# The first feed-forward's first layer moved into the last attention batch of a two-layer gated cross-attention kernel

## The chip, the cores and the metric

The kernel runs on one core of one Trainium2 chip. The time is the device time of the whole launch, in microseconds, as the median of several runs. Profiled executions give a trace of every instruction of the engines: TensorE (PE, its weight loads PEld), VectorE (DVE), ScalarE (ACT), GpSimd (POOL) and the DMA queues.

## The reference, cut to what matters

Four residual blocks run one after the other on x (8 batches of 100 tokens, 256 wide). Only the first block is touched here:

```
xn  = layernorm(x)
q   = xn @ Wq + bq                       # 16 heads of 16
k,v = ctx @ Wk + bk, ctx @ Wv + bv       # ctx: 8 x 361 x 192
out = softmax(q k^T / 4) v               # 8 x 100 x 256
h   = relu(out @ W1 + b1)                # 256 -> 512
x   = x + tanh(g) * (h @ W2 + b2)        # 512 -> 256
```

After it come a mixture of 8 experts with top-1 routing, a cross-attention with ternary weights and int8-rounded activations on the same context, and a mixture of 16 attention projections. The context projections of the third block don't depend on x. Two of their layers are woven into the attention rounds of the first block as "chain units".

## The kernel before, in words

Every engine's stream is written out by hand, in one order, with semaphores between the engines. All matrices named here are fp32.

The attention of the first block runs in ten rounds, n = 0 to 9 (`for n in range(B + 2)`, once in the ACT block and once in the PE block). Round n works on batch n: `turn_maxima(n)` turns the row maxima, and then twelve steps u take one group of four heads and a third of the context each. At even u the PE runs `score_pair(n, u)` (four fp32 products at L1761 and two bf16 ones at L1767) for steps u and u + 1, and where `EXTRA[n]` has one a `chain_unit` (L1704 in round 7). ACT turns each step's scores into probabilities with an exponential (L1414). Scores, chain units and the turned maxima share three banks, so the PE may only be three results ahead of ACT. At u = 6 and 10 the PE computes `values(n - 1, ..)` of the batch before (L1779) into bank 7. ACT copies that bank at its own u = 10 (`zo`, L1409), the PE turns it (`turn_values(n - 1)`, L1791), DVE divides by the sums (`normalise`, L750 and L751), the PE turns the result back in the next round at u = 2 (`turn_heads(n - 2)`, L1798), and ACT adds the bias and stores it in `qT` (`heads_out`, L1380). `values(b)` waits for `heads_out(b - 1)`.

Rounds 8 and 9 have no scores of their own. Only values and turns of the last batches are left in them.

The feed-forward follows. `first_product(half, m)` is the first layer for four batches (half 0: batches 0 to 3) and a quarter m of the 512 hidden columns: two k-steps of 128x400 in fp32, four instructions in the trace (L1608, weights from `w_1`, seen as `region` and `w_a`). `hidden_out(n)` is ACT's relu of it into `h0T` (L1390). `second_layer(b)` is the second layer for one batch: four k-steps of 100x256, eight instructions (L1608, `stage<-stage`, seen as `bank<-stage`), into bank b % 4. From b = 4 on it waits for `x1_done` b - 3, which is DVE's residual of batch b - 4.

In the kernel before, the four `first_product(0, m)` and their `hidden_out` stand in rounds 8 and 9 between the turns. `second_layer(0)` stands behind round 9. Then the PE waits for the last `heads_out`, runs `first_product(1, 0..3)` and then `second_layer(1)` to `second_layer(7)`, with `turn_tokens_half(2, 0)` (L1602) after `second_layer(6)`.

On DVE, the order after round 8's `normalise(7)` is fixed: the scale of the third block's activations (L723, a reduction over partitions on POOL, L625 to L632), the rounding of the whole context (`quantise(qc, ctx_a, ctx_a, 8)`, L642 and L643 on 128x5776), the bias of the residual (L834), and only then, batch after batch:

```
for b in range(B):
    dve.wait_ge(S["y0_mm"], b + 1)
    dve.scalar_tensor_tensor(x[:, b, :], psum[b % 4]..., x[:, b, :]).then_inc(S["x1_done"], 1)
    dve.wait_ge(S["x1_done"], b + 1)
    ins = token_stats(b)
```

(L838 and L556.) After b = 3 it computes the variance of the first half. ACT normalises those four batches (L1283), the PE turns them, and so on to the router.

`h0T` lies over the part of the stage tile in which the projected values of earlier batches lie. Its first 400 columns touch those of batch 6, whose `values` are run in round 7.

Of the kernel before, what the change touches and what calls it, by code (L numbers as in the profile page):

```python
# [17 lines left out]
B, N, D = 8, 100, 256  # L18
# [119 lines left out]
def flamingo(nc, d):  # L138

    ctx = ExitStack()  # L140
    with ctx:
# [3 lines left out]
        def sem(name):  # L145
            return ctx.enter_context(nc.semaphore(name))
# [34 lines left out]
        def raw(name):  # L181
            p, w, _ = TERN[name]
            home = stage if name == "f1" else region
            return home[0:p, RAW[name]:RAW[name] + w]

        def weight(name):
            p, w, at = TERN[name]
            return tern[0:p, at:at + w]
# [67 lines left out]
        def cut_r(n):  # L256
# [62 lines left out]
        S = {n: sem(n) for n in (  # L319
            "small_in", "x_in", "raw_in", "ctx_in0", "ctx_in1", "ctx_in2", "ctx_in3", "ctx_in4", "consts_in", "w_q_in", "ffn_in", "w_abs", "tern_ready",  # L320
            "ln_var", "ln_std", "ln_out", "ln_turned", "xT_ready",
            "max_part", "max_all", "quantised", "kv_mm", "kv_out", "xn_stored", "placed", "inverse_mm", "inverse_done", 
            "q_mm", "q_out", 
            "pv_mm", "o_out",
            "h0_mm", "h0_out", "y0_mm", "x1_done",
            "logit_mm", "logit_a", "logit_e", "onehot_done", "rank_mm", "te_done", "zeroed",
            "w1_in0", "w1_in1", "w2_in0", "w2_in1", "xs_in0", "xs_in1", "xs_turned", "xs_out",
# [932 lines left out]
        def _(act):  # L1260
# [82 lines left out]
            def f1_magnitude(part):  # L1343

                at_p = slice(1024 * part, 1024 * part + 1024)
                if part == 0:
                    act.wait_ge(S["large_in"], 16)
                act.activation(weight("f1")[:, at_p], raw("f1")[:, at_p], ACT.Abs,
                               accum_out=scol[:, 48 + part:49 + part]).then_inc(S["large_abs"], 1)
# [26 lines left out]
            def heads_out(b):  # L1376

                act.wait_ge(S["f_mm"], b + 1)
                for k in range(2):
                    act.activation(qT[:, k, b * N:(b + 1) * N], psum[7][:, k * N:(k + 1) * N], ACT.Identity,  # L1380
                                   bias=cols[:, COLS["bv"] + k:COLS["bv"] + k + 1]).then_inc(S["o_out"], 1)
# [4 lines left out]
            def hidden_out(n):  # L1386

                half, m = n // 4, n % 4
                act.wait_ge(S["h0_mm"], n + 1)
                act.activation(h0T[:, m, half * HT:(half + 1) * HT], psum[n][:, 0:HT], ACT.Relu,  # L1390
                               bias=cols[:, 4 + m:5 + m]).then_inc(S["h0_out"], 1)

            for n in range(B + 2):
                if n < B:
                    act.wait_ge(S["y_mm_a"], FIRST[n] + 1)
                    act.copy(nmT[n % 2], psum[4 + FIRST[n] % 3][:, 0:200].bitcast(BF16)).then_inc(S["y_out_a"], 1)
                if n == B:
                    hidden_out(0)
                if n == B + 1:
                    hidden_out(2)  # L1400
                    hidden_out(3)
                for u in range(12):
                    if u == 2 and n >= 2:
                        heads_out(n - 2)
                    if u == 4 and n == B:
                        hidden_out(1)
                    if u == 10 and 1 <= n <= B:
                        act.wait_ge(S["pv_mm"], n)
                        act.copy(zo, psum[7][:, 0:4 * N]).then_inc(S["zo_out"], 1)  # L1409
                    if n < B:  # L1410
                        c, g = u // 4, u % 4
                        rows_c, y = CH[c][1], UNIT[n, u]
                        act.wait_ge(S["y_mm_a"], y + 1)
                        act.activation(probsT[n % 2][0:rows_c, c, g].rearrange("p j n -> p (j n)"),  # L1414
                                       psum[4 + y % 3][0:rows_c, 0:4 * N], ACT.Exp).then_inc(S["y_out_a"], 1)
                        if u % 2 == 1 and u // 2 < len(EXTRA[n]):
                            chain_out(*EXTRA[n][u // 2])
                        if (n, u) in TOTAL:
                            total_out(n, u)
                        if n == 3 and u % 3 == 2:  # L1420
                            f1_magnitude(u // 3)

            for n in range(4, 8):
                hidden_out(n)
# [148 lines left out]
        def _(pe):  # L1573
# [32 lines left out]
            def layer(bank, w, src, halves, kk, start=True, stop=True):  # L1606
                for k in range(kk):
                    ins = pe.matmul(bank, w(k), src(k), start=start and k == 0, stop=stop and k == kk - 1)  # L1608
                return ins
# [114 lines left out]
            def score_wave(b, w):  # L1724

                t, par = w // 2, w % 2
                if w == 0:
                    pe.wait_ge(S["qm_done"], b + 1)
                for i in range(4):
                    if (b, w, i) == (0, 1, 2):  # L1730
                        pe.wait_ge(S["sum_read"], 1)
                    if 4 * b + w > 0 and i % 2 == 0:
                        pe.wait_ge(S["x_max"], 2 * (4 * b + w - 1) + i // 2 + 1)
                    at_i = slice(32 * i, 32 * i + 32)
                    ins = pe.matmul(psum[i + (4 if b == 0 else 0)][0:N, 0:M], qm[b % 3][at_i, t, 2 * (i % 2) + par, :], kT[at_i, t, b, :],  # L1735
                                    start=True, stop=True)
                    if i % 2 == 1:
                        ins.then_inc(S["x_mm"], 1)
# [78 lines left out]
            def first_product(half, m):  # L1817

                at_h = slice(half * HT, (half + 1) * HT)
                layer(psum[4 * half + m][:, 0:HT], lambda k: w_1[k][:, m * P:(m + 1) * P], lambda k: qT[:, k, at_h], 2, 2)\  # L1820
                    .then_inc(S["h0_mm"], 1)

            def second_layer(b):

                if b >= 4:
                    pe.wait_ge(S["x1_done"], b - 3)
                layer(psum[b % 4][0:N, 0:D], lambda k: h0T[:, k, b * N:(b + 1) * N],
                      lambda k: w_2[:, k, :], 1, 4).then_inc(S["y0_mm"], 1)

            for n in range(B + 2):  # L1830
                if n + 1 < B:
                    score_wave(n + 1, 0)
                if n < B:
                    turn_maxima(n)
                if n == B:
                    pe.wait_ge(S["ffn_in"], 32)
                    pe.wait_ge(S["x_max"], 8 * B)
                    first_product(0, 0)
                if n == B + 1:
                    first_product(0, 3)  # L1840
                for u in range(12):
                    if u == 2 and n >= 2:
                        turn_heads(n - 2)
                    if u == 4 and n + 1 < B:
                        score_wave(n + 1, 1)
                    if u == 4 and n == B:
                        first_product(0, 1)
                    if u in (6, 10) and 1 <= n <= B:
                        values(n - 1, u // 2 - 3)
                        values(n - 1, u // 2 - 2)  # L1850
                    if u in (6, 8) and n + 1 < B:
                        score_wave(n + 1, u // 2 - 1)
                    if n < B and u % 2 == 0:
                        score_pair(n, u)
                        if u // 2 < len(EXTRA[n]):
                            chain_unit(*EXTRA[n][u // 2])
                        if (n, u + 1) in TOTAL:
                            total_unit(n, u + 1)
                if n == B:
                    first_product(0, 2)  # L1860
                if 1 <= n <= B:
                    turn_values(n - 1)
            pe.wait_ge(S["h0_out"], 4)
            pe.wait_ge(S["w1_small_in"], 16)
            second_layer(0)

            pe.wait_ge(S["o_out"], 2 * B)
            for m in range(4):
                first_product(1, m)
            for b in range(1, B):  # L1870
                if b == 4:
                    pe.wait_ge(S["h0_out"], 8)
                second_layer(b)
                if b == 6:
                    turn_tokens_half(2, 0)
# [120 lines left out]
            for n in range(2 * B + 4):  # L1996
                if n < 2 * B:
                    a, b = n // B, n % B
# [24 lines left out]
                if n >= 4:  # L2023
                    g = n - 4
                    a, b = g // B, g % B
# [251 lines left out]
```

## Time and profile before

| | us |
|---|---|
| median of 3 runs | 611.55 (610.88 to 611.57) |
| the profiled execution | 610.34 |
| its span | 608.5 |
| PE busy in the span | 591.6 (97%) |
| DVE busy | 325.9 (54%) |
| ACT busy | 218.4 (36%) |

Times in the profile count from the span's start. Round 7 is at 166.7 to 179.9, rounds 8 and 9 at 179.9 to 189, the rest of the feed-forward up to 209. A timeline row merges neighbouring instructions of one kind. Its start and the start of the next row are exact, while the duration of a PE row includes the drain of its last matmul, so that two rows overlap by some 0.1 to 0.2 us. A busy PE may still stand waiting between two such matmuls.

### The profile page before, as it was taken

The page shows a single profiled execution, that of the slowest core. Times are in us where ns is not written, and L with a number is a line of the kernel's source. Part 1 is how long each engine was busy: PE and PEld are TensorE (multiplying, and loading weights), DVE is VectorE, ACT ScalarE, POOL GpSimd, SP SyncE. Part 2 cuts the span into 40 slices and gives each one's busy share as a digit, 9 for nine tenths or more (in the row PEclk, how much of TensorE's full clock was granted, in tenths as well). Part 3 has the DMA queues.
Part 4 walks back from the last instruction along what each step waited for, and adds up shares of the span by engine and source line. Part 5 has one row for each costly group of instructions (what it writes and reads, how often), then busy time and mean ns, then how long its engine had stood idle before and what let it go on. Part 6 is the DMA issues. An engine that isn't in the chain of part 4 may idle for free.

```text
span 608.5 us, 9623 instructions
## 1 busy us (share of the span) xinstructions
PE 591.6 (97%) x3759; PEld 405.6 (67%) x3759; DVE 325.9 (54%) x787; ACT 218.4 (36%) x511; POOL 75.9 (12%) x75
## 2 busy tenths in 40 slices
PE   9999999999999999999999889999999999999997
PEld 7656344454556777999999558677655555555587
DVE  1996767597876655222222779886362223131454
ACT  3554665756663364121112476662200010001000
POOL 0052201013006203222221000001001000000000
PEclk9999999999999969999999999999999999999999
DMA  8920000102001644999996000601733833220000
GB/s 185 301 107 1 18 1 1 37 2 57 1 1 39 227 169 132 336 345 330 335 341 226 15 2 12 231 2 27 245 101 89 310 104 93 89 78 1 0 28 27
DMA packets 25580, 70.63 MB, mean 116 GB/s; under 512 B 5255, under 2 KB 13031, under 8 KB 21703
## 3 DMA queue, kind: packets, MB, share of 16 engines
q1 hardware_dynamic: 21910, 58.16, 29.3%
q0 software_dynamic: 3632, 11.97, 6.0%
q8 instruction: 25, 0.41, 0.3%
q14 instruction: 13, 0.10, 0.0%
HBM read 64.62 MB, written 5.49 MB: 115 GB/s over the span
## 4 chain that ended last, share of the span: by engine, by line
PE 85%; DVE 6%; ACT 5%; DMA 2%; issue 1%; SPq 1%; POOL 0%; DVEq 0%
PE bank L2112 21%; PE bank L1608 10%; PE bank L1932 8%; PE bank L1945 8%; PE bank L1761 7%; PE bank L2148 7%; PE bank L1735 5%; PE bank L1779 3%; DMA region<-in_ctxT 2%; PE bank L1704 2%; ACT region L1500 2%; PE bank L1767 2%; PE bank L2066 1%; PE bank L1589 1%; DVE nmax L1033 1%
## 5 line engine op out<-in xcount | busy, mean ns | idle before, releaser
L2112 PE MATMUL bank<-region,kvT 128*128 128x400 f32 x384 | 130.4, 500 | 0.0
L2112 PEld LDWEIGHTS bank<-region,kvT 128*128 128x128 f32 x384 | 72.5, 190 | 54.1 <-issue 0.3
L731 DVE TENSOR_REDUCE nmax<-bank 100x2 f32<-100x722 f32 x64 | 55.2, 905 | 24.2 <-PE bank L1735 23.9
L1174 DVE TENSOR_TENSOR region<-xT,stage 128x800 f32<-128x800 f32 x30 | 29.7, 991 | 70.1 <-PE bank L2112 70.0
L1932 PEld LDWEIGHTS bank<-stage,region 128*128 128x128 f32 x448 | 52.1, 192 | 1.4 <-issue 0.8
L1932 PE MATMUL bank<-stage,region 128*128 128x128 f32 x448 | 52.4, 276 | 0.5 <-ACT stage L1435 0.5
L1945 PE MATMUL bank<-region,stage 128*128 128x256 f32 x224 | 50.7, 380 | 0.0
L1945 PEld LDWEIGHTS bank<-region,stage 128*128 128x128 f32 x224 | 41.5, 190 | 5.0
L2148 PE MATMUL bank<-region,kvt 128*128 128x200 f32 (+1 forms) x192 | 44.5, 389 | 0.3 <-DVE region L1200 0.3
L1458 ACT ACTIVATE stage<-bank,stage 128x128 f32<-128x128 f32 x56 | 16.0, 368 | 67.5 <-PE bank L1932 36.5
L2148 PEld LDWEIGHTS bank<-region,kvt 128*128 128x128 f32 x192 | 33.5, 190 | 9.3 <-DVE region L1200 0.6
L1761 PE MATMUL bank<-xT,kvt 64*121 64x400 f32 (+1 forms) x144 | 38.2, 545 | 0.7 <-ACT region L1414 0.4
L947 DVE TENSOR_SCALAR stage<-bank,stage 128x128 f32<-128x128 f32 x56 | 15.8, 345 | 43.1 <-PE bank L1932 43.1
L1200 DVE TENSOR_TENSOR region<-region,stage 128x200 f32<-128x200 f32 (+1 forms) x48 | 20.5, 435 | 31.3 <-PE bank L2148 31.3
L1414 ACT ACTIVATE region<-bank 121x400 f32<-121x400 f32 (+1 forms) x48 | 21.6, 501 | 20.7 <-PE bank L1767 20.7
L1414 ACT ACTIVATE kvT<-bank 121x400 f32<-121x400 f32 (+1 forms) x48 | 21.8, 501 | 18.1 <-PE bank L1767 18.1
L953 DVE TENSOR_TENSOR stage<-bank,stage 128x256 f32<-128x256 f32 x14 | 5.9, 425 | 35.7 <-PE bank L1945 35.7
L1735 PE MATMUL bank<-kvt,xT 32*100 32x361 f32 x192 | 23.6, 502 | 0.7 <-ACT stage L1305 0.5
L1608 PE MATMUL bank<-region,w_a 96*128 96x361 f32 x64 | 21.2, 475 | 1.6 <-DMA region<-in_ctxT 0.9
L1761 PEld LDWEIGHTS bank<-xT,kvt 64*121 64x121 f32 (+1 forms) x144 | 13.4, 178 | 14.0 <-ACT region L1414 3.6
L1536 ACT ACTIVATE region<-bank 128x400 f32<-128x400 f32 x6 | 2.6, 504 | 55.5 <-PE bank L2112 55.5
L1608 PE MATMUL bank<-w_a,region 96*121 96x256 f32 (+1 forms) x96 | 22.1, 381 | 0.0
(352 smaller groups left out, 931.7 us busy)
## 6 DMA issues: line engine op xcount, KB each, us to landing
region<-in_e_w SPq DMA_DIRECT2D x28, 1024.0 KB, 5.8
kvT<-in_p_qkv SPq DMA_DIRECT2D x32, 384.0 KB, 3.1
stage<-w_dram POOLq DMA_DIRECT2D x2, 1600.0 KB, 12.7
stage<-in_t_f SPq DMA_DIRECT2D x1, 2048.0 KB, 15.6
kvt<-in_p_o SPq DMA_DIRECT2D x1, 2048.0 KB, 10.1
stage<-in_e_b SPq DMA_DIRECT2D x14, 128.0 KB, 7.9
region<-in_ctxT SPq DMA_DIRECT2D x3, 541.5 KB, 14.9
stage<-w_dram POOLq DMA_DIRECT2D x1, 1200.0 KB, 8.8
```

What stands on the lines that cost most here:

```text
L731: dve.tensor_reduce(nmax[:, b % 2, at_h:at_h + 9:8], banks[0:N, bank:bank + 2, 0:M], AX.X, ALU.max, negate=True)\
L1174: dve.tensor_tensor(x_w[n % NW], xT[:, :, at_h], w_bc[h][:, None, e, :].to_broadcast([P, 2, HT]), ALU.mult).then_inc(S["xw_done"], 1)
L1200: dve.tensor_tensor(z_w[n % NW][:, at_p], oT[h][:, at_p], w_bc[h][:, e, at_p], ALU.mult)\
L1414: act.activation(probsT[n % 2][0:rows_c, c, g].rearrange("p j n -> p (j n)"), psum[4 + y % 3][0:rows_c, 0:4 * N], ACT.Exp).then_inc(S["y_o ...
L1608: ins = pe.matmul(bank, w(k), src(k), start=start and k == 0, stop=stop and k == kk - 1)
L1735: ins = pe.matmul(psum[i + (4 if b == 0 else 0)][0:N, 0:M], qm[b % 3][at_i, t, 2 * (i % 2) + par, :], kT[at_i, t, b, :], start=True, stop= ...
L1761: pe.matmul(bank[g], kT[at_g, t, b, c0:c0 + rows_c], qm[b % 3][at_g, t].rearrange("p j n -> p (j n)"), start=True, stop=False)
L1779: ins = pe.matmul(psum[7][32 * i:32 * i + VW, w * N:(w + 1) * N], v_b[b][0:rows_c, c, 8 * t + 2 * i + par, :], probsT[b % 2][0:rows_c, c, ...
L1932: ins = pe.matmul(psum[2 * u + m // 4][:, (m % 4) * P:(m % 4 + 1) * P], e_w1[u][:, k, m * P:(m + 1) * P], xsT[u][:, k, :], start=k == 0, s ...
L1945: ins = pe.matmul(psum[4 + u][:, 0:D], hsT[u][:, m, :], e_w2[u][:, m, :], start=m == 0, stop=m == KF - 1)
L2112: ins = pe.matmul(psum[3 * h + j][:, 0:HT], p_w[n % NP][:, k, j * HE:(j + 1) * HE], x_w[n % NW][:, k, :], start=e == 0 and k == 0, stop=e ...
L2148: ins = pe.matmul(psum[LAST_BANK[part] + m][:, at_p], o_all[:, e, m * P:(m + 1) * P], z_w[n % NW][:, at_p], start=e == 0, stop=e == E1 - 1)
```

## The change

The four `first_product(0, m)` move from rounds 8 and 9 into round 7: one after `turn_maxima(7)`, the others at u = 4, 6 and 8 ahead of the step's values and scores. Their `hidden_out` move into ACT's round 7: 1 at u = 6, 2 at u = 8, 0 after the copy of bank 7 at u = 10, and 3 after the last step. In their old places stand `second_layer(0)` to `second_layer(3)`. Behind round 9 the PE runs `first_product(1, 0..3)` and then only `second_layer(4)` to `second_layer(7)`.

```diff
 # ACT
-                if n == B:
-                    hidden_out(0)
-                if n == B + 1:
-                    hidden_out(2)
-                    hidden_out(3)
                 for u in range(12):
                     if u == 2 and n >= 2:
                         heads_out(n - 2)
-                    if u == 4 and n == B:
+                    if u == 6 and n == B - 1:
                         hidden_out(1)
+                    if u == 8 and n == B - 1:
+                        hidden_out(2)
                     if u == 10 and 1 <= n <= B:
                         act.wait_ge(S["pv_mm"], n)
                         act.copy(zo, psum[7][:, 0:4 * N]).then_inc(S["zo_out"], 1)
+                    if u == 10 and n == B - 1:
+                        hidden_out(0)
...
+                if n == B - 1:
+                    hidden_out(3)
 # PE
-                if n == B:
+                if n == B - 1:
                     pe.wait_ge(S["ffn_in"], 32)
                     pe.wait_ge(S["x_max"], 8 * B)
                     first_product(0, 0)
+                if n == B:
+                    pe.wait_ge(S["h0_out"], 4)
+                    pe.wait_ge(S["w1_small_in"], 16)
+                    second_layer(0)
                 if n == B + 1:
-                    first_product(0, 3)
+                    second_layer(3)
                 for u in range(12):
                     if u == 2 and n >= 2:
                         turn_heads(n - 2)
                     if u == 4 and n + 1 < B:
                         score_wave(n + 1, 1)
+                    if u in (4, 6, 8) and n == B - 1:
+                        first_product(0, u // 2 - 1)
                     if u == 4 and n == B:
-                        first_product(0, 1)
+                        second_layer(1)
...
                 if n == B:
-                    first_product(0, 2)
+                    second_layer(2)
                 if 1 <= n <= B:
                     turn_values(n - 1)
-            pe.wait_ge(S["h0_out"], 4)
-            pe.wait_ge(S["w1_small_in"], 16)
-            second_layer(0)
 
             pe.wait_ge(S["o_out"], 2 * B)
             for m in range(4):
                 first_product(1, m)
-            for b in range(1, B):
-                if b == 4:
-                    pe.wait_ge(S["h0_out"], 8)
+            pe.wait_ge(S["h0_out"], 8)
+            for b in range(4, B):
                 second_layer(b)
                 if b == 6:
                     turn_tokens_half(2, 0)
```

## Rows read from the trace of the kernel before

**Rows 1.** The page, part 1: busy us, share of the span, instructions.

```profile
PE 591.6 (97%) x3759; PEld 405.6 (67%) x3759; DVE 325.9 (54%) x787; ACT 218.4 (36%) x511; POOL 75.9 (12%) x75
```

**Rows 2.** The chain that ended last, from round 9 on: start us, us, what.

```profile
188.52 0.60 ACT stage L1390
...
189.17 17.70 PE bank L1608 x72
```

**Rows 3.** Timeline of PE in round 7: start us, us, instructions [idle before].

```profile
167.01 1.23 PE L1761 MATMUL bank<-xT,kvt 64*121 64x400 f32 x3
...
168.67 0.48 PE L1704 MATMUL bank<-stage,tern 128*128 128x361 bf16 x2
...
169.25 1.24 PE L1761 MATMUL bank<-xT,kvt 64*121 64x400 f32 x4
...
170.59 0.48 PE L1704 MATMUL bank<-stage,tern 128*128 128x361 bf16 x2
...
171.09 0.99 PE L1761 MATMUL bank<-xT,kvt 64*121 64x400 f32 x3
...
172.52 0.48 PE L1704 MATMUL bank<-stage,tern 128*128 128x361 bf16 x2
...
174.10 0.94 PE L1761 MATMUL bank<-xT,kvt 64*121 64x400 f32 x4
...
175.13 0.48 PE L1704 MATMUL bank<-stage,tern 128*128 128x361 bf16 x2
...
175.79 0.99 PE L1761 MATMUL bank<-xT,kvt 64*119 64x400 f32 x3 [0.17 <-ACT kvT L1414]
...
177.21 1.25 PE L1779 MATMUL bank<-region,stage 121*17 121x100 f32 x48
...
179.42 0.65 PE L1791 MATMUL bank<-consts,kvT 128*100 128x128 f32 x4
```

**Rows 4.** Timeline of ACT at the end of round 7 and in round 9.

```profile
178.52 0.49 ACT L1409 COPY kvT<-bank 128x400 f32<-128x400 f32 x1 [0.46 <-PE bank L1779]
179.52 0.90 ACT L1414 ACTIVATE kvT<-bank 119x400 f32<-119x400 f32 x2 [0.51 <-PE bank L1767]
...
189.01 0.57 ACT L1380 ACTIVATE xn<-bank,cols 128x100 f32<-128x100 f32 x2
```

**Rows 5.** Timeline of PE in rounds 8 and 9 and behind them.

```profile
179.90 0.84 PE L1608 MATMUL bank<-xn,region 128*128 128x400 f32 x2
...
186.54 0.60 PE L1791 MATMUL bank<-consts,kvT 128*100 128x128 f32 x4
...
190.97 0.84 PE L1608 MATMUL bank<-xn,region 128*128 128x400 f32 x2
...
196.35 10.52 PE L1608 MATMUL bank<-stage 128*100 128x256 f32 x48
```

**Rows 6.** Timeline of DVE, ACT and PE from the rounding of the context on.

```profile
189.82 3.22 DVE L642 TENSOR_SCALAR region<-region,scol 128x5776 f32<-128x5776 f32 x1
...
198.74 0.48 DVE L838 SCALAR_TENSOR_TENSOR x<-bank,tg,x 100x256 f32<-100x256 f32 x1
...
201.73 0.48 DVE L838 SCALAR_TENSOR_TENSOR x<-bank,tg,x 100x256 f32<-100x256 f32 x1 [0.35 <-PE bank L1608]
...
203.97 2.07 ACT L1283 ACTIVATE xn<-x,var,rstd 100x256 f32<-100x256 f32 x4 [0.44 <-DVE var L587]
...
207.40 1.89 PE L1608 MATMUL bank<-stage 128*100 128x256 f32 x8
```

**Rows 7.** Windows: us, busy (x instructions) of PE, PEld, DVE, ACT, POOL, granted PE clock, DMA share, GB/s.

```profile
210.39:213.80 3.41, 1.58 (x11) 0.94 (x10) 1.36 (x7) 2.21 (x6) 0.00 (x0) 1.00 0.84 286
213.80:217.20 3.40, 3.39 (x19) 3.09 (x20) 0.45 (x3) 1.25 (x1) 0.00 (x0) 0.50 0.74 259
217.20:220.60 3.40, 3.40 (x17) 2.63 (x16) 1.84 (x10) 2.15 (x6) 0.00 (x0) 0.50 0.83 303
220.60:224.05 3.45, 3.45 (x15) 2.49 (x14) 3.08 (x21) 2.73 (x6) 0.00 (x0) 0.50 0.25 90
346.90:350.30 3.40, 2.99 (x12) 2.18 (x13) 2.53 (x9) 2.47 (x7) 0.35 (x1) 0.50 0.00 0
```

## The prediction

> **What bounds the kernel now.** I first read the page for the engines' shares: the PE is busy 97% of the span and DVE 54% [rows 1]. So PE work that only changes its place costs what it cost before, unless it lands in a stretch where the PE stands waiting. What matters is where it waits, before and after. Next I read the chain that ended last. From round 9 on it is PE alone except for one ACT relu: 17.70 us of L1608 in one piece, which is seven second layers and four first products [rows 2]. Third, I read the timelines of PE, ACT and DVE around the change, since a busy PE row can hide a wait between two matmuls. There the reader is to see two things. First, in round 7 the PE is held up for short times by ACT, though the page calls it busy. Second, DVE starts its long rounding right behind round 8 and comes to the first residual only at 198.74 [rows 6].
>
> **Two chains start at turn_values(7).** It ends at 187.14 in round 8 (186.54 + 0.60) [rows 5]. One chain is the PE's: first_product(0, 3), turn_heads(7), eight second layers, four first products and one turn of tokens, 22.15 us until second_layer(7) ends at 209.29 (207.40 + 1.89) [rows 6]. The other is DVE's: normalise(7), the scale, 2 x 3.2 us of rounding, the bias, then the residuals of batches 0 to 3, their variance, ACT's normalisation, the turn of tokens and second_layer(7). Before, the PE's chain is the later one, and the DVE's has little slack. The first residual starts 11.60 us behind turn_values(7). The fourth starts at 201.73 after 0.35 us of waiting for the PE, and, counting back the rest of its delay, could have started 0.4 us earlier at the pace of 0.86 us a batch. ACT's four normalisations end at 206.04 (203.97 + 2.07) [rows 6], and would end at 205.6. The turn of tokens needs about 0.45 us behind the last of them, so second_layer(7) could start at 206.1 instead of 207.40. **The slack of DVE's chain is 1.3 us.** Whatever delays turn_values(7) by more than that makes the kernel slower, however much the PE's tail behind it shrinks.
>
> **Part 1, four first products into round 7.** The four of half 1 run back to back from 190.97 to 196.35, so 5.38 us, 1.35 each [rows 5]. What they can fill is the waiting in round 7. A score pair without a wait takes 1.03 us from its first matmul to the next kind (174.10 to 175.13). Pair 0 takes 1.66 (+0.63), pair 2 1.34 (+0.31), pair 4 1.43 (+0.40). Pair 8 starts 0.26 late (0.40 after the chain unit at 175.13 would be 175.53) and takes 1.42, so +0.65 [rows 3]. That is 1.99 us in the round. Three of the four products stand right ahead of pairs 0, 4 and 8 and give ACT the time it lacked there, so I take 1.68 as filled. The 0.31 of pair 2 stays, and first_product(0, 2), ahead of values and pair 6, has no wait to fill. ACT's three relus at u = 6, 8 and 10 cost it 0.5 to 0.6 us each [rows 2]. It has that time, as the PE gives it 1.35 us more at each place. Cost: 5.38 - 1.68 = **+3.70**. Bounds: all 1.99 filled gives +3.4; nothing filled gives +5.4.
>
> **Part 2, second_layer(0) waits for hidden_out(3).** It stands in first_product(0, 0)'s old place, which started at 179.90 right behind turn_values(6) [rows 5]. It needs all four quarters of the hidden layer, and the last relu is queued on ACT behind both last exponentials. ACT copies bank 7 at 178.52 (0.49), then runs the new hidden_out(0) (to 179.50). The exponentials start at 179.52 as before and end at 180.42 [rows 4], and hidden_out(3) ends at 181.02. So the PE, which waited for nothing here, waits from 179.90 to 181.05: **+1.15**. Behind the wait stand turn_heads(6), heads_out(6) and with it values(7). Bounds: 0.9 if ACT's operations run closer, 1.3 if the exponentials come later. The 0.51 us wait of the old second_layer(0) goes away, but it lay behind turn_values(7) and buys nothing on DVE's chain.
>
> **Part 3, second layers for first products in round 8.** Six second layers take 10.52, 1.75 each [rows 5]. Three of them, 0 to 2, stand ahead of turn_values(7) where three first products of 1.35 stood: 3 x 0.40 = **+1.2**. They cover the same hand-overs (normalise(6) to turn_heads(6), the copy of bank 7) with room to spare, so no wait comes or goes.
>
> **Sum at turn_values(7):** 3.70 + 1.15 + 1.2 = 6.05. It ends at 193.2 instead of 187.14.
>
> **Part 4, the tail.** Behind it the PE now has second_layer(3) 1.75, turn_heads(7) 0.17, a wait for heads_out(7) of about 0.6 (its 0.57 [rows 4] no longer lies under second_layer(0)), and four first products 5.38: 7.9 us. Then it waits for h0_out 8 (0.6), and then second_layer(4) waits for x1_done 1, which comes 12.1 us behind turn_values(7) (11.60 + 0.48) [rows 6]. So **the PE stands idle for 4.2 us**, at about 201.1 to 205.3. Before, second_layer(1) to (3) covered this. The end is then DVE's chain: second_layer(7) ends at 209.29 + 6.05 - 1.3 = 214.0, **+4.75 us**. Second layers 4 to 6 run from 205.3 to 210.5, and the turn of tokens isn't ready before 211.7, so they have 1.2 us to spare. Everything behind (router, experts) starts from that end and moves with it. The DMAs of expert weights start from the end of the rounding and from x1_done 8, so they move too, and come no later relative to their users.
>
> **Part 5, the clock.** In the trace the granted clock fell from 1.00 to 0.50 (2.4 to 1.2 GHz) at 213.80, after 3.41 us in which the PE was busy 1.58 us, and stayed there for 10.25 us, of short router products first. After another fall it was back in 3.4 us, at 350.3, under denser work [rows 7]. An idle stretch of 4.2 us is worse than what went ahead of these falls, so I expect a third one, around second_layer(4). Each us at half clock is half a us of PE work. For about 2 us it is lost in the 1.2 us to spare. If it lasts 5.5 us it costs 2.7 - 1.2 = 1.5, and if it lasts as long as the one at 213.80, the rest of the feed-forward doubles: 6.9 + 0.7 us more, less 1.2, so about +6. Weighing these by how dense fp32 second layers are, nearer to the fall at 346.90, I take **+0.5**. (The Trainium skill, TensorE: Matmul & The Clock Gate, in its part on the HAM clock gate, says that the throttled state is the default and that only recent activity releases it. By that rule the fall is certain, and the sum would be 4.75 plus 1 to 2 us. The rows agree on the fall after sparse work. No row has an idle stretch as long.)
>
> **The time.** 610.34 + 4.75 + 0.5 = 615.6 for an execution like the profiled one. The median of the runs lies 1.2 above that one, so 616.8.
>
> **Rivals.**
>
> *A, the same chain, but a long fall of the clock.* The place and the price are those of part 5: +3.5 to +6 above the warm sum, so 619.8 to 622.5. For it: the fall at 213.80 lasted 10.25 us. Against it: those were router products of 8 columns. Chance 0.13.
>
> *B, a smaller loss.* Round 7's fillable waits are larger than I read them, for instance because ACT's delays spread over every pair, and hidden_out(3) is earlier: 3.4 + 0.9 + 1.2 - 1.3 = 4.2 with the counted waits, and with another us filled 3.2, so 614.7, and no fall of the clock. Chance 0.12.
>
> *C, on the other side: the new products cost the PE nothing in round 7.* If ACT and not the PE set the pace of round 7, the four products would slip into its shadow. Then turn_values(7) comes 1.2 later by the second layers alone, which is DVE's slack, the result is 611.5, and without the wait for hidden_out(3) it would be slightly faster. It decides at a delay of turn_values(7) below 1.3 us, for which 5.38 us would have to vanish, against 1.99 us of waits that I can find [rows 3]. If DVE's chain were not the end, the PE would only lose its waits: 2 us filled and 0.5 saved against 1.15, 0.6 and 0.6 new ones, so 611.4. Chance of both together 0.05, split between same and faster.
>
> **How the numbers follow.** The forecast (PE delay of 6.05, DVE's chain as the end, clock fall short) has 0.70 and spans 615.3 to 618.8: 3.9 to 5.9 for the sum by the bounds of parts 1 and 2, and 0 to 1.5 for the clock. With B and half of A the range that holds 8 in 10 is 614.5 to 620.0. About 0.2% (1.2 us) is what a measurement of this kernel can tell from no change. Slower by more has 0.70 + 0.13 + 0.12 = 0.95, within it 0.03, faster 0.02.
>
> **What the profile after would show.** Round 7 from turn_maxima to the end of turn_values(6) is 3.7 us longer, with pairs 0, 4 and 8 at about 1.03. A PE wait of about 1.1 us ahead of second_layer(0) on ACT L1390. L750 of batch 7 at about 193.2. A PE wait of about 4 us ahead of second_layer(4), put down to DVE x L838 (this is the row that tells most). L838 without waits for batches 0 to 3, 0.86 apart. The chain through DVE L642, L643, L834, L838 where PE L1608 stood. A granted clock of 0.5 beginning between 203 and 207. I am wrong if turn_values(7) comes less than 1.3 us later, or if the wait ahead of second_layer(4) is missing. The size is off if the clock stays down longer than some 5 us.

## The result, and the profile after

The changed kernel takes 618.72 us (median of 4 runs, 617.41 to 621.20) against 611.21 us before (4 runs, 609.76 to 611.57). The ratio is 1.0123, with a 95% interval of 1.0097 to 1.0149: 7.5 us slower. The profiled execution took 617.41 us with a span of 615.6 us, 7.1 us longer than before.

The page of the changed kernel, part 1 and the clock row of part 2. The engines' busy time hardly moved (PE 591.6 to 594.2, [rows 1]), so it gives no hint of where 7 us went. The clock row gives one: ahead of the 6 that the row before had too (the fall of 213.80 [rows 7]) there is now a 7, for the slice from 200.1 to 215.5 us. The two 8s further right are the fall that stood at 346.90 before. It lasted 6.83 us here instead of 3.41, and as long in e1 below, which takes the time of the kernel before, so it is not the loss.

```profile
PE 594.2 (97%) x3759; PEld 406.4 (66%) x3759; DVE 325.7 (53%) x787; ACT 218.4 (35%) x511; POOL 76.6 (12%) x75
...
PEclk9999999999999769999999889999999999999999
```

The timeline of PE in the changed kernel (start us, us, instructions, idle before it). Round 7 starts with the turned maxima at 167.09. Every score pair (L1762) now runs without a wait except the one at 170.47.

```profile
167.09 0.34 PE L1749 MATMUL bank<-ident_bf,small 100*128 100x100 bf16 x4
167.27 0.90 PE L1609 MATMUL bank<-xn,region 128*128 128x400 f32 x2
...
168.77 0.94 PE L1762 MATMUL bank<-xT,kvt 64*121 64x400 f32 x4
...
169.81 0.48 PE L1705 MATMUL bank<-stage,tern 128*128 128x361 bf16 x2
...
170.47 0.99 PE L1762 MATMUL bank<-xT,kvt 64*121 64x400 f32 x3
...
171.89 0.48 PE L1705 MATMUL bank<-stage,tern 128*128 128x361 bf16 x2
...
183.64 0.64 PE L1792 MATMUL bank<-consts,kvT 128*100 128x128 f32 x4
185.17 1.97 PE L1609 MATMUL bank<-stage 128*100 128x256 f32 x8 [0.89 <-ACT stage L1390]
...
192.99 0.60 PE L1792 MATMUL bank<-consts,kvT 128*100 128x128 f32 x4
...
196.16 0.94 PE L1609 MATMUL bank<-xn,region 128*128 128x400 f32 x2 [0.67 <-ACT xn L1380]
...
205.82 7.89 PE L1609 MATMUL bank<-stage 128*100 128x256 f32 x24 [4.02 <-DVE x L838]
213.55 0.85 PE L1603 MATMUL bank<-consts,xn 100*128 100x100 f32 x8
214.24 1.89 PE L1609 MATMUL bank<-stage 128*100 128x256 f32 x8
```

Pair 0 (168.77 to 169.81) takes 1.04 us where it took 1.66 [rows 3]. The reader is to see three waits: 0.89 us ahead of second_layer(0), which had one of 0.51 before, but behind turn_values(7) and not ahead of it; 0.67 ahead of the first products of half 1, which is new; and 4.02 ahead of second_layer(4), new too and put down to DVE's first residual. Second layers 4 to 6 then take 7.73 us (205.82 to 213.55), where the same three take 5.26 in e1 and e3 below. The windows of the changed kernel around them show why (us, busy of PE, PEld, DVE, ACT, POOL, granted clock, DMA share, GB/s):

```profile
200.64:204.05 3.41, 1.16 (x4) 0.37 (x2) 3.41 (x4) 2.32 (x3) 3.41 (x3) 1.00 0.28 52
204.05:210.88 6.83, 5.06 (x12) 3.59 (x13) 6.16 (x18) 1.12 (x3) 3.32 (x5) 0.50 0.96 351
210.88:214.24 3.36, 3.36 (x22) 2.68 (x22) 1.39 (x3) 1.31 (x4) 0.00 (x0) 1.00 0.41 138
```

The granted clock was half from 204.05 to 210.88 (and again from 221.12 to 231.36, where the kernel before had the fall of 213.80 [rows 7]). For the first 1.77 us of the new fall the PE still stood idle. The other 5.06 us lie on the second layers.

DVE's side of the changed kernel, to be read against [rows 6]: the quotient of batch 7, both rounding passes, the bias, the first, second, fourth and eighth residuals.

```profile
193.63 0.26 DVE L750 RECIPROCAL recip<-bank 100x16 f32<-100x16 f32 x1 [8.52 <-PE bank L1792]
...
196.27 3.22 DVE L642 TENSOR_SCALAR region<-region,scol 128x5776 f32<-128x5776 f32 x1
199.53 3.21 DVE L643 TENSOR_SCALAR stage<-region 128x5776 bf16<-128x5776 f32 x1
...
202.81 2.34 DVE L834 SCALAR_TENSOR_TENSOR x<-rows,tg,x 100x2048 f32<-100x2048 f32 x1
205.19 0.48 DVE L838 SCALAR_TENSOR_TENSOR x<-bank,tg,x 100x256 f32<-100x256 f32 x1
...
206.05 0.47 DVE L838 SCALAR_TENSOR_TENSOR x<-bank,tg,x 100x256 f32<-100x256 f32 x1
...
207.74 0.47 DVE L838 SCALAR_TENSOR_TENSOR x<-bank,tg,x 100x256 f32<-100x256 f32 x1
...
216.17 0.48 DVE L838 SCALAR_TENSOR_TENSOR x<-bank,tg,x 100x256 f32<-100x256 f32 x1 [1.12 <-PE bank L1609]
```

The first residual starts 11.56 us behind L750, as before (187.18 to 198.74, the latter in [rows 6]), and DVE stood idle for 8.52 us just ahead of L750. The last one starts at 216.17; before, at 209.33, as these two rows of the kernel before show:

```profile
187.18 0.26 DVE L750 RECIPROCAL recip<-bank 100x16 f32<-100x16 f32 x1 [6.29 <-PE bank L1791]
...
209.33 0.48 DVE L838 SCALAR_TENSOR_TENSOR x<-bank,tg,x 100x256 f32<-100x256 f32 x1 [1.13 <-PE bank L1608]
```

That is 6.84 of the 7.1 us of the span. The rest of the program is as long as it was, 0.2 us apart.

### The profile page after: what moved, and what is told of

It reads as the page before. It is cut to its first block, busy times and chain, and to the rows that moved or that the text cites. A ratio compares the mean times of both kernels' runs of the same rounds, so it can differ in the third digit from the quotient of the medians.

```text
span 615.6 us, 9623 instructions
## 1 busy us (share of the span) xinstructions
PE 594.2 (97%) x3759; PEld 406.4 (66%) x3759; DVE 325.7 (53%) x787; ACT 218.4 (35%) x511; POOL 76.6 (12%) x75
## 4 chain that ended last, share of the span: by engine, by line
PE 83%; DVE 7%; ACT 5%; DMA 2%; issue 2%; POOL 1%; SPq 1%; DVEq 0%
PE bank L2115 21%; PE bank L1609 9%; PE bank L1935 8%; PE bank L1948 8%; PE bank L1762 7%; PE bank L2151 7%; PE bank L1736 5%; PE bank L1780 3%; DMA region<-in_ctxT 2%; PE bank L1705 2%; ACT region L1501 2%; PE bank L1768 2%; PE bank L2069 1%; PE bank L1590 1%; DVE nmax L1033 1%
## 5 line engine op out<-in xcount | busy, mean ns | idle before, releaser
L1762 PE MATMUL bank<-xT,kvt 64*121 64x400 f32 (+1 forms) x144 | 36.9, 545 | 0.5 <-ACT region L1413 0.4
L1609 PE MATMUL bank<-stage 128*100 128x256 f32 x64 | 17.5, 429 | 4.9 <-DVE x L838 4.0
```

The costliest lines, as they stand in the source:

```text
L1762: pe.matmul(bank[g], kT[at_g, t, b, c0:c0 + rows_c], qm[b % 3][at_g, t].rearrange("p j n -> p (j n)"), start=True, stop=False)
```

## The experiments

All were timed beside the kernel before, whose median was 611.90 us beside e1 to e4, 611.07 beside e5 to e8 and 610.99 beside e9. The changed kernel stands with its first four runs. So a difference of two medians of different groups can be off by some 0.9 us, and the ratio is the safer number. Two moments in each trace tell nearly everything: the start of L750 for batch 7 (when turn_values(7) ends) and the start of the eighth residual (when second_layer(7) ends). The clock column is the fall ahead of the eighth residual, if there was one.

| kernel | L750 | 8th residual | distance | clock fall | median us | ratio to before, 95% |
|---|---|---|---|---|---|---|
| before | 187.18 | 209.33 | 22.15 | none | see above | |
| changed | 193.63 | 216.17 | 22.54 | 6.83 us | 618.72 | 1.0123 [1.0097, 1.0149] |
| e1 | 193.31 | 209.98 | 16.67 | none | 612.34 | 1.0009 [0.9984, 1.0033] |
| e2 | 187.15 | 209.24 | 22.09 | none | 611.03 | 0.9981 [0.9963, 0.9999] |
| e3 | 193.37 | 214.26 | 20.89 | none | 616.68 | 1.0072 [1.0045, 1.0098] |
| e4 | 192.63 | 214.37 | 21.74 | 3.41 us | 616.30 | 1.0070 [1.0047, 1.0093] |
| e5 | 187.54 | 210.74 | 23.20 | none | 613.13 | 1.0026 [1.0005, 1.0047] |
| e6 | 191.60 | 212.50 | 20.90 | none | 615.31 | 1.0057 [1.0035, 1.0080] |
| e7 | 192.22 | 208.89 | 16.67 | none | 610.74 | 0.9989 [0.9968, 1.0009] |
| e8 | 191.31 | 207.35 | 16.04 | none | 609.34 | 0.9976 [0.9953, 1.0000] |
| e9 | 191.30 | 213.03 | 21.73 | 3.41 us | 614.84 | 1.0059 [1.0030, 1.0088] |

**e1 and e2: DVE's rounding earlier.** The scale and the first pass of the rounding move ahead of `normalise(7)`, on the changed kernel (e1) and on the kernel before (e2). The second pass and the bias stay behind it.

```diff
+            def scale_and_first_pass():
+                chain_scale(1, 8)
...
+                link(dve.tensor_scalar(ctx_a, ctx_a, scol[:, 11:12], MAGIC, ALU.mult, ALU.add))
...
+                if n == B:
+                    scale_and_first_pass()
                 if n >= 1:
                     normalise(n - 1)
...
-            quantise(qc, ctx_a, ctx_a, 8).then_inc(S["quantised"], 1)
+            dve.tensor_scalar(qc, ctx_a, MAGIC, None, ALU.subtract).then_inc(S["quantised"], 1)
```

> The changed kernel, with the scale and the first pass of the context rounding moved on DVE ahead of normalise(7), where DVE stands idle. Theory A (DVE's chain behind turn_values(7) sets the end): the first residual comes some 5 us earlier, the 4.0 us wait ahead of second_layer(4) and the fall of the clock there are gone, and second_layer(7) ends at about 209.8 against 209.3 before and 216.1 in the changed kernel. Time 611.7, about 7 us below the changed kernel. Theory B (the loss is PE time and waits in rounds 7 and 8): nothing of that moves, 617 to 619.

> The same move on DVE in the kernel before. Theory A: the PE's chain is the later one there, so the time stays within 0.5 us of before. If moving the rounding were a gain by itself, it would be 1 us or more faster here too, and run e1 would say less.

DVE and PE in e1 (timeline):

```profile
186.64 3.22 DVE L795 TENSOR_SCALAR region<-region,scol 128x5776 f32<-128x5776 f32 x1
193.31 0.26 DVE L750 RECIPROCAL recip<-bank 100x16 f32<-100x16 f32 x1 [3.46 <-PE bank L1798]
...
199.56 0.48 DVE L844 SCALAR_TENSOR_TENSOR x<-bank,tg,x 100x256 f32<-100x256 f32 x1
...
209.98 0.48 DVE L844 SCALAR_TENSOR_TENSOR x<-bank,tg,x 100x256 f32<-100x256 f32 x1 [1.12 <-PE bank L1615]
```

```profile
202.10 5.42 PE L1615 MATMUL bank<-stage 128*100 128x256 f32 x24 [0.68 <-ACT stage L1396]
```

The wait of 4.02 us and the fall of the clock are gone together, and the three second layers take 5.26 us (202.10 to 207.36, and 5.42 with the drain of the last one). Of the wait ahead of second_layer(4) only the 0.68 us for hidden_out(7) are left. The waits ahead of second_layer(0) and of the first products of half 1 stay. The time comes back by some 6.4 us to that of the kernel before, with turn_values(7) as late as in the changed kernel (193.31). So it is through DVE's chain that the later turn_values(7) costs its time. Without that chain in the way the eighth residual is only 0.65 us later than before. In e2 the same edit moves the eighth residual by 0.1 us. Its ratio, 0.9981 with an interval that just leaves out 1, is at the limit of what can be told. The move is worth 6 us only where the change stands.

**e3: no fall of the clock.** The extra products compute nothing that is used.

```diff
             pe.wait_ge(S["h0_out"], 8)
+            keep_busy(4, 7)
             for b in range(4, B):
```

> The changed kernel with seven extra 128x256 fp32 products into a free bank ahead of second_layer(4), 3.0 us of filling for an idle stretch of 4.0 us. Theory A: the granted clock stays at 1.00 until after second_layer(7), which ends 1.7 us earlier, at 214.4; time 1.7 us below the changed kernel, 617.0. Theory C (the fall of the clock is most of the loss): it comes back to within 2 us of before, 611 to 613.

PE in e3, the filling and the second layers behind it, then the windows:

```profile
202.23 3.29 PE L1590 MATMUL bank<-consts 128*128 128x256 f32 x14 [0.69 <-ACT stage L1390]
205.47 5.42 PE L1609 MATMUL bank<-stage 128*100 128x256 f32 x24
```

```profile
200.71:205.47 4.76, 4.07 (x17) 2.77 (x16) 4.69 (x6) 2.00 (x3) 4.76 (x6) 1.00 0.42 120
205.47:214.26 8.79, 8.42 (x44) 6.37 (x44) 6.50 (x24) 3.17 (x7) 1.66 (x3) 1.00 0.73 274
```

The clock stays at full rate and the distance from L750 to the eighth residual is 20.89 instead of 22.54: **the fall cost 1.65 us**. The time is 2.0 below the changed kernel by the medians, 3.1 by the ratios, and 1.0072 of before. Theory C (the fall of the clock is most of the loss) is out: with the clock at full rate 4.93 of the 6.84 us at the eighth residual remain, and by the ratios six tenths of the loss.

**e4: the last relu earlier.**

```diff
                     if u == 10 and n == B - 1:
                         hidden_out(0)
+                        hidden_out(3)
...
-                if n == B - 1:
-                    hidden_out(3)
```

> The changed kernel with hidden_out(3) ahead of the last two exponentials of round 7 instead of behind them. Theory A: the 0.89 us wait ahead of second_layer(0) shrinks to about 0.1, turn_values(7) and all behind it come 0.8 us earlier: 617.9. If the wait were covered elsewhere: no change.

PE in e4: second_layer(0) follows turn_values(6) without a recorded wait.

```profile
183.55 0.65 PE L1791 MATMUL bank<-consts,kvT 128*100 128x128 f32 x4
184.17 1.97 PE L1608 MATMUL bank<-stage 128*100 128x256 f32 x8
```

L750 comes 1.0 us earlier than in the changed kernel. The eighth residual comes 1.8 earlier, since here the clock fell only from 205.69 to 209.10, which cost 0.85 (21.74 - 20.89). The median is 2.4 lower where 0.8 was expected. The extra is of the size of the spread from run to run (below), so the runs confirm the direction and the trace the 1.0.

**e5: the slack of DVE's chain.** A reduction of 2.40 us, its result unused, in the kernel before.

```diff
+            dve.tensor_reduce(lmax[:, 0:1], ctx_a[0:N, :, 0:3, :], AX.XYZ, ALU.max)
             chain_scale(1, 8)
```

> The kernel before with one extra DVE reduction of about 2.3 us ahead of the scale of the third block, its result unused. It measures the slack of DVE's chain. Theory A (slack 1.3 us): the turn of tokens waits and second_layer(7) ends 1.0 us later, time +1.0. With no slack: +2.3. With 2.3 us or more of slack: no change.

DVE in e5:

```profile
187.54 0.26 DVE L750 RECIPROCAL recip<-bank 100x16 f32<-100x16 f32 x1 [6.29 <-PE bank L1792]
...
188.17 2.40 DVE L816 TENSOR_REDUCE lmax<-region 100x1 f32<-100x2166 f32 x1
...
201.42 0.48 DVE L839 SCALAR_TENSOR_TENSOR x<-bank,tg,x 100x256 f32<-100x256 f32 x1
...
210.74 0.48 DVE L839 SCALAR_TENSOR_TENSOR x<-bank,tg,x 100x256 f32<-100x256 f32 x1 [1.68 <-PE bank L1609]
```

The first residual moves 2.32 us away from L750 (13.88 against 11.56), the eighth only 1.05 (23.20 against 22.15). The slack was 1.27 us. The median is 2.1 above before, 1.6 by the ratio, whose interval holds the 1.05.

**e6: second layers 1 to 3 behind the first products of half 1**, the first layers staying in round 7 and second_layer(0) in round 8.

```diff
-                if n == B + 1:
-                    second_layer(3)
...
-                        second_layer(1)
...
-                if n == B:
-                    second_layer(2)
...
-            pe.wait_ge(S["h0_out"], 8)
-            for b in range(4, B):
+            for b in range(1, B):
+                if b == 4:
+                    pe.wait_ge(S["h0_out"], 8)
```

> The changed kernel with only the first layers moved: second layers 1 to 3 stand behind first_product(1, 3) again, second_layer(0) stays in round 8. Theory A: turn_values(7) ends 2.4 us earlier than in the changed kernel (3.5 us less work, 1.1 us of hand-overs without cover), at 191.2; the PE has work until x1_done 1, so no fall of the clock; second_layer(7) ends at about 212.2. Time about 4 us below the changed kernel, 614.5, and 3 above before. Theory B (all of the loss is the first layers in round 7 and the order doesn't matter): as the changed kernel.

L750 comes 2.0 us earlier than in the changed kernel. That is less than the 3.5 us of second layers 1 and 2 that no longer stand ahead of it, since the hand-overs now have no cover, as these rows of PE show:

```profile
188.04 2.28 PE L1780 MATMUL bank<-kvT,stage 121*17 121x100 f32 x96 [0.76 <-ACT xn L1380]
190.93 0.64 PE L1792 MATMUL bank<-consts,kvT 128*100 128x128 f32 x4 [0.60 <-ACT kvT L1406]
192.38 0.39 PE L1799 MATMUL bank<-consts,tmp 100*128 100x100 f32 x2 [0.81 <-DVE tmp L751]
193.44 0.94 PE L1609 MATMUL bank<-xn,region 128*128 128x400 f32 x2 [0.67 <-ACT xn L1380]
```

These are 2.84 us of waits on the PE, of which only the last 0.67 is there in the changed kernel too, and yet this kernel is 3.4 us faster than the changed one: the wait of 4.02 us ahead of second_layer(4) is filled. The eighth residual follows L750 by 20.90 us, the same as in e3. That is the clearest sight of DVE's chain: in two kernels with quite different PE orders, and full clock in both, the end comes 20.9 us behind turn_values(7).

**e7, e8 and e9: the change mended.** e7 has the edits of e1 and e4. e8 has those and cuts second layers 2 and 3 into halves of two k-steps. e9 is e8 without the move on DVE.

```diff
+            def second_part(b, ks):
+                for k in ks:
+                    ins = pe.matmul(psum[b % 4][0:N, 0:D], h0T[:, k, b * N:(b + 1) * N], w_2[:, k, :],
+                                    start=k == 0, stop=k == 3)
+                if ks[-1] == 3:
+                    ins.then_inc(S["y0_mm"], 1)
...
-                    second_layer(3)
+                    second_part(2, (2, 3))
...
-                    second_layer(2)
+                    second_part(2, (0, 1))
...
+            second_part(3, (0, 1))
             pe.wait_ge(S["o_out"], 2 * B)
             for m in range(4):
                 first_product(1, m)
+            second_part(3, (2, 3))
             pe.wait_ge(S["h0_out"], 8)
```

> Both edits of e1 and e4 in the changed kernel. Theory A: PE's chain is the end, so the 0.8 us of the earlier relu come on top: 610.9. If DVE's chain still were the end, no better than e1.

> e7 with second layers 2 and 3 each cut in two halves of two k-steps, so that one half (0.87 us) covers each of the four hand-overs: the copy of bank 7, normalise(7), heads_out(7), hidden_out(7). Theory A: the waits of 0.67 us ahead of first_product(1, 0) and 0.6 us ahead of second_layer(4) go, 1.2 us below e7, 609.7, which would be below the kernel before by 1.5.

> The PE and ACT order of e8 (relu 3 early, second layers 2 and 3 in halves) without the move on DVE. Theory A: turn_values(7) ends where it did in e8 (L750 of batch 7 at 191.3), DVE's chain of 20.9 us behind it sets the end, so the eighth residual starts at 212.2 and not at 207.4 as in e8, some 3 us later than before: 614 to 615, with the PE idle ahead of second_layer(4) again and a fall of the clock possible. If the PE's order alone were the gain of e8, the time would be 609 to 610 here too.

PE in e8 has no recorded wait from the values of batch 7 to second_layer(4) at 199.49:

```profile
190.61 0.60 PE L1797 MATMUL bank<-consts,kvT 128*100 128x128 f32 x4
191.04 1.03 PE L1839 MATMUL bank<-stage 128*100 128x256 f32 x4
192.09 0.39 PE L1804 MATMUL bank<-consts,tmp 100*128 100x100 f32 x2
192.31 1.03 PE L1839 MATMUL bank<-stage 128*100 128x256 f32 x4
193.18 0.91 PE L1614 MATMUL bank<-xn,region 128*128 128x400 f32 x2
...
198.63 1.03 PE L1839 MATMUL bank<-stage 128*100 128x256 f32 x4
199.49 1.74 PE L1614 MATMUL bank<-stage 128*100 128x256 f32 x7
```

PE in e9, with the same order and the same L750, waits again:

```profile
203.50 7.08 PE L1608 MATMUL bank<-stage 128*100 128x256 f32 x24 [3.86 <-DVE x L838]
```

e8 is the fastest of all: 609.34, and its eighth residual starts 2.0 us earlier than before. By the ratio (0.9976, interval up to 1.0000) it is 1.5 us faster than the kernel before, just at the limit of what can be told. e9 is 614.84. The PE order that is 1.5 us better than before with DVE's chain out of the way is 3.6 us worse than before with it.

## Why the prediction was right

It said 616.8 us in a range of 614.5 to 620.0, and slower with a chance of 0.95. The main reason, DVE's chain behind turn_values(7), held: e1 takes it out of the way and the loss is gone, e5 lengthens it in the kernel before and the end moves. The forecast was 1.9 us too low, most of it in the clock. The start of round 7 in the kernel before, which part 1 needs beside [rows 3]:

```profile
166.71 0.34 PE L1748 MATMUL bank<-ident_bf,small 100*128 100x100 bf16 x4
```

The terms against the traces:

- *Part 1*, the first products in round 7: +3.70 forecast. From the turned maxima to turn_values(6) it was 12.71 us before (166.71 to 179.42) and is 16.55 now (167.09 to 183.64), so +3.84. The pair that was said to keep its wait kept it (1.42 at 170.47). That the sum came out so close is in part luck. The four products took 5.82 us up to the start of what follows them (1.50 at 167.27, then three times 1.44), not 5.38, and what they filled was then 1.98, not 1.68.
- *Part 2*, the wait for hidden_out(3): +1.15 forecast. Second_layer(0) starts 1.53 us behind the start of turn_values(6) where first_product(0, 0) started 0.48 behind it [rows 3, 5]: +1.05. e4 took it out and gained 1.0.
- *Part 3*: +1.2 forecast. From the start of that product to turn_values(7) it was 6.64 [rows 5] and is 7.82: +1.18.
- *Sum at turn_values(7)*: 6.05 forecast, 6.07 measured. L750 comes 6.45 later, of which 0.38 were there before round 7 began and are not the change's. (Such an offset also lies between traces of one PE order: L750 is at 193.63 in the changed kernel, 193.31 in e1 and 193.37 in e3.)
- *Slack of DVE's chain*: 1.3 forecast, 1.27 by e5, and 1.25 as the difference of 22.15 and 20.90.
- *Part 4*, the idle stretch ahead of second_layer(4): 4.2 forecast, 4.02 recorded.
- *Part 5*, the clock, is the term that was mis-sized. The fall came where it was expected, with a cost of +0.5 put on it. It lasted 6.83 us in the profiled execution and cost 1.65 (e3). I had taken it to be like the fall of 3.4 us at 346.90 and let 1.2 us of spare time absorb it. Second layers 4 to 6 took 2.47 us more than in e3 (7.73 against 5.26), and 1.65 of that reached the end, so the spare time was 0.8 us and not 1.2. In e4 and e9 the fall lasted 3.41 us and cost 0.85 and 0.83. There the three took 6.92 and 6.91 us, 1.66 and 1.65 more than in e3, of which again 0.8 was absorbed. The Trainium skill's rule (TensorE: Matmul & The Clock Gate, the part on the HAM clock gate), that the throttled state is the default and activity only releases it, agrees with this trace: with the idle stretch filled in e3, no fall came there. The 1 to 2 us that the prediction named beside that rule was the better size. A fall ahead of the eighth residual came in all three traces with such an idle stretch (the changed kernel, e4, e9) and in none of the others.

Together: 0.38 + 6.07 - 1.25 + 1.65 = 6.85, against 6.84 measured at the eighth residual. The 1.25 and the 1.65 are differences between these same moments in e3 and e6, so the agreement is no test of its own; e5's 1.27 is the measurement from another side.

One line of the prediction doesn't follow from its parts: the bounds of parts 1 and 2 give 4.2 to 6.6 for the sum without the clock, not 3.9 to 5.9. The measured 4.82 (6.07 - 1.25) lies in both.

Rival A (a long fall) didn't come in the profiled execution, though the run of 621.2 us lies in its range. There is no trace of that run, only its mean clock, 0.977 against 0.981, so where its extra time at half rate lay is open. Rival B (a smaller loss and no fall of the clock) was right that more waiting could be filled than was counted on (1.98 against 1.68, though pair 2 kept its wait, so a part lay in short gaps between the pairs). But the products took longer, hidden_out(3) was not early enough (+1.05 and not +0.9), and the fall came. Rival C is refuted by the +3.84, and its second form, in which DVE's chain is not the end, by e1 and e5. What stays open is the last 0.4 us between the medians' difference (7.5) and the traces' (7.1), which is less than the spread of the runs.

## What to carry to other kernels

When work is moved forward into a stretch where it costs little, ask what it delays. Here the moved products came ahead of the hand-over that starts a long, fixed chain on another engine, and that chain had 1.3 us of slack for a delay of 6. The test is a sum of two chains from their common start, one for each engine, and it can be done on the trace before the change. The same move can pay once the other engine's part is taken out of its way, which here was 5 us of work beside an idle stretch of 8.5.

A new wait on TensorE can cost more than its length. Here the clock fell in it, the work behind ran at half rate for 5.06 us, and that took up the 0.8 us of spare time and cost 1.65 us more.

## What the runs showed of the hardware that was not expected

Runs of one kernel differ, and in some kernels they do so with the mean granted clock. In e2's twelve runs, 609.51, 609.52, 609.74 and 610.19 us went with a mean clock of 0.992, 610.66 to 611.10 (and one of 612.40) with 0.986, 612.05, 612.48 and 612.78 with 0.983, and 613.41 with 0.980. A span of 610 us at 0.992 has 2 x 0.008 x 610 = 9.8 us at half rate, one at 0.980 has 24.4. So 14.6 us more at half rate went with 3.9 us more time. The falls in the traces came in lengths of 3.41, 6.83, 10.24 and 13.65 us, for stretches of the program that are the same: the one behind the router lasted 10.24 us before and in the changed kernel and 13.65 in e1, e2, e5 and e6. The relation isn't as clean elsewhere. In e5 the runs with a mean of 0.983 spread from 612.14 to 615.14 us, and in e8 one run took 612.09 at 0.986 and another 609.24 at 0.983. So time at half rate goes with a part of the spread of 2 to 4 us between runs of one kernel, and what makes the rest is open. Changes of 1 us are lost in it and were read from the traces here.
